# Reordering the gated feed-forward stage of a fused two-layer block: the second half's normalisation and weights pass ahead of the first half's epilogue

## What is computed

```
x = x + attn_like(layernorm(x))          # state-space mixer, then GELU MLP
x = x + ffn(layernorm(x))                # gated feed-forward

attn_like(x):
    xn = layernorm(x)*w + b
    gate, gate_gate = silu(xn @ gate_w + gate_b) split in two
    u = (xn*gate) @ state_w + state_b ;  Bm = gate_gate @ state_w + state_b
    delta = softplus(mean(xn @ state_w + state_b))
    y[t] = exp(-delta)*y[t-1] + delta*Bm*u
    x = x + y @ out_w + out_b
    return x + gelu(layernorm(x) @ mlp_w1 + b1) @ mlp_w2 + b2

ffn(x):                                   # weights are int, times 1/127
    h = silu(x @ w_gate.T) * (x @ w_up.T)           # hidden width 3072
    return h @ w_down.T
```

## Time and profile before

| what | value |
|---|---|
| runs shown | 7316.8 us and 8023.67 us, median 7670.24 us |
| profiled execution, its own time | 7320.83 us |
| span of its slowest core (core 6) | 7319.0 us |
| spans of the eight cores | 7274.2 to 7319.0 us |
| PE busy | 5569.8 us, 76% of the span |
| DVE busy | 2215.0 us, 30% |
| ACT busy | 1357.7 us, 19% |
| mean granted TensorE clock | 0.911 to 0.916 of full |

### The profile page before, as it was taken

The page is one execution under the profiler, slowest core; times in us unless marked ns, Lnnn a source line. Parts: engine busy times, 40 slices in busy tenths (PEclk is TensorE's granted clock), DMA queues, the critical chain, the costliest instruction groups (busy, mean ns, idle before and its releaser), DMA issues.

```text
span 7319.0 us, 70654 instructions; the slowest of 8 cores (7274.2 to 7319.0 us)
## 1 busy us (share of the span) xinstructions
PE 5569.8 (76%) x25312; PEld 2644.4 (36%) x25792; DVE 2215.0 (30%) x3924; ACT 1357.7 (19%) x1880; POOL 13.1 (0%) x28
## 2 busy tenths in 40 slices
PE   0027788769887688877888698877888778886988
PEld 0013344324433344433443344333444334433443
DVE  0024123340344213441233403442134502334033
ACT  0012111222112211121112221122112221122211
POOL 0000000000000000000000000000000000000000
PEclk9998899889998899988999799988999889987999
DMA  9940324211341124402242114411244022421143
GB/s 108 109 93 24 104 82 134 106 69 53 123 151 54 64 80 124 147 23 104 82 133 108 69 58 122 157 44 74 70 131 140 24 104 90 140 93 69 64 125 123
DMA packets 161078, 690.51 MB, mean 94 GB/s; under 512 B 18978, under 2 KB 19107, under 8 KB 134820
## 3 DMA queue, kind: packets, MB, share of 16 engines
q1 hardware_dynamic: 156964, 608.37, 25.3%
q0 software_dynamic: 3776, 77.60, 6.5%
HBM read 696.38 MB, written 77.59 MB: 106 GB/s over the span
## 4 chain that ended last, share of the span: by engine, by line
PE 69%; DVE 11%; DMA 6%; another core or an unknown queue 6%; issue 5%; ACT 3%; DVEq 0%; SPq 0%; ACTq 0%; POOL 0%; POOLq 0%
PE pb L334 27%; PE pb L916 12%; PE pb L1100 9%; PE pb L1088 9%; PE pb L1179 7%; DMA REG<-s_mlp 3%; PE pb L386 2%; DMA REG<-s_fd 2%; PE pb L413 2%; DVE REG L731 1%; ACT TTR L1019 1%; PE pb L668 1%; DVE X L777 1%; DVE TTR L779 1%
## 5 line engine op out<-in xcount | busy, mean ns | idle before, releaser
L334 PE MATMUL pb<-FMB,REG 128*128 128x512 bf16 x4000 | 895.0, 384 | 321.6 <-DMA REG<-s_mlp 314.5
L386 PE MATMUL pb<-IDF,TTR 128*128 128x128 f32 x1536 | 293.9, 342 | 861.8 <-DVE TTR L510 501.0
L916 PE MATMUL pb<-M1R,TTR 128*128 128x512 bf16 x4016 | 884.2, 379 | 14.1 <-ACT M1R L350 8.8
L334 PE MATMUL pb<-REG,M1R 128*128 128x512 bf16 x3008 | 701.5, 394 | 144.7 <-DVE REG L737 140.0
L1179 PE MATMUL pb<-M1R,REG 128*128 128x512 bf16 x3008 | 688.3, 387 | 71.8 <-DMA REG<-s_fd 46.8
L1088 PE MATMUL pb<-FMB,REG 128*128 128x512 bf16 x3008 | 719.7, 379 | 21.1 <-DVE FMB L1034 18.5
L1100 PE MATMUL pb<-FMB,REG 128*128 128x512 bf16 x3008 | 719.7, 379 | 3.5
L334 PEld LDWEIGHTS pb<-FMB,REG 128*128 128x128 bf16 x4096 | 403.7, 99 | 809.1 <-issue 339.5
L932 DVE TENSOR_SCALAR TTR<-pb,CB_M 128x512 f32<-128x512 f32 x128 | 96.1, 751 | 1977.5 <-PE pb L916 1977.5
L916 PEld LDWEIGHTS pb<-M1R,TTR 128*128 128x128 bf16 x4096 | 400.6, 98 | 495.0 <-issue 16.8
L386 PEld LDWEIGHTS pb<-IDF,TTR 128*128 128x128 f32 x1536 | 217.6, 175 | 938.7 <-issue 928.5
(11 more groups left out here) (97 smaller groups left out, 2938.6 us busy)
## 6 DMA issues: line engine op xcount, KB each, us to landing
TTR<-s_mlp SPq DMA_DIRECT2D x128, 1024.0 KB, 4.9
REG<-s_fg SPq DMA_DIRECT2D x384, 256.0 KB, 2.7
REG<-s_fu SPq DMA_DIRECT2D x384, 256.0 KB, 2.7
REG<-s_fd SPq DMA_DIRECT2D x128, 768.0 KB, 4.5
TTR<-x_in SPq DMA_DIRECT2D x16, 2048.0 KB, 8.9
M1R<-s_gate SPq DMA_DIRECT2D x8, 4096.0 KB, 12.8
y_out<-X POOLq DMA_DIRECT2D x16, 2048.0 KB, 6.6
s_mlp<-w_mlp POOLq DMA_DIRECT2D x2, 8192.0 KB, 175.6
```

The lines of the kernel that those rows point to most:

```text
L334: ins = t.matmul(psum[bank][:, 0:512], wsb[:, w_tile(m, k) * P:(w_tile(m, k) + 1) * P], rhs_fn(s, k), start=(k == 0), stop=(k == n_k - 1))
L386: ins = t.transpose(psum[bank][:, tau * P:(tau + 1) * P], src[:, tau * 1024 + c * P: tau * 1024 + (c + 1) * P], IDF[:])
L916: ins = t.matmul(psum[bank][:, 0:512], A_RING[:, slot + k * P:slot + (k + 1) * P], M1[:, k * 512:(k + 1) * 512], start=(k == 0), stop=(k = ...
```

## The change

```diff
-            for s in range(NSUB):
+            def emit_ln3(s, t2_free):
...
-                    for mk in reg_free["T2"]:
+                    for mk in t2_free:
...
+            def emit_gu(s, zn_marks, m1_free):
...
-                    if s == 0:
-                        pr.waits(t, "pe", reg_free["M1"])
+                    pr.waits(t, "pe", m1_free)
...
                         if m > 0:
                             pr.wait(ac, "act", ("dve", dve_base3 + (m - 1) * 2 + 2))
+                        elif CM.get(f"hlast{b}_{1 - s}") is not None and s == 1:
+                            pr.wait(ac, "act", CM[f"hlast{b}_0"])
...
                         pr.wait(dv, "dve", CM[f"fuf{b}_{s}_{m}"])
+                        if s == 1 and m == 0:
+                            pr.wait(dv, "dve", CM[f"fdf{b}_0_{ND - 1}"])
...
-                if s == 1 and b + 1 < n_blocks:
-                    emit_A_chain(b + 1, 0, defer_x1gen=False)
...
-                if s == 1 and b + 1 < n_blocks:
-                    wmix_free_next = pr.mark("pe")
-                    reg_free["FMB"] = [ffn_gu_done]
-                    emit_A_tail_sub(b + 1, 0, pending_xn[0])
-                    emit_A_chain(b + 1, 1, defer_x1gen=True)
...
+            emit_ln3(0, reg_free["T2"])
+            zn0, _ = emit_zn(0)
+            h0 = emit_gu(0, zn0, reg_free["M1"])
+            emit_ln3(1, [pr.mark("pe")])
+            zn1, _ = emit_zn(1)
+            d0base = emit_down(0, h0)
+            ffno0 = emit_fev4(0, d0base)
+            h1 = emit_gu(1, zn1, [])
+            ffn_gu_done = pr.mark("pe")
+            if b + 1 < n_blocks:
+                emit_A_chain(b + 1, 0, defer_x1gen=True)
+            emit_ffn_tail(0, ffno0)
+            if b + 1 < n_blocks:
+                emit_X1gen(b + 1, 0)
+            d1base = emit_down(1, h1)
+            ffno1 = emit_fev4(1, d1base)
+            if b + 1 < n_blocks:
+                wmix_free_next = pr.mark("pe")
+                reg_free["FMB"] = [ffn_gu_done]
+                emit_A_tail_sub(b + 1, 0, pending_xn[0])
+                emit_A_chain(b + 1, 1, defer_x1gen=True)
+            emit_ffn_tail(1, ffno1)
+            reg_free["M1"] = [pr.mark("pe")]
+            if b + 1 < n_blocks:
+                emit_X1gen(b + 1, 1)
+                emit_A_tail_sub(b + 1, 1, pending_xn[1])
```

More of the change, by code:

```diff
@@ L982, in build_program @@
             rds = [12288, 15360]
-            for s in range(NSUB):
+            ringslots_d = rds
+            def emit_ln3(s, t2_free):
                 def fv7(dv, s=s):
@@ L1010, in build_program, with fa8 @@
                 dve_sec(fv7)
-                def fa8(ac, s=s):
+                def fa8(ac, s=s, t2_free=t2_free):
                     pr.wait(ac, "act", CM[f"ln3c{b}_{s}"])
-                    for mk in reg_free["T2"]:
+                    for mk in t2_free:
                         pr.wait(ac, "act", mk)
@@ L1025, in build_program, with emit_zn @@
                 act_sec(fa8)
+            def emit_zn(s):
                 fills4 = tm_to_fm_pe(T2, [CM[f"t3{b}_{s}"]], "dve")
@@ L1040, in build_program @@
                 dve_sec(fev_zn)
-                reg_free["T2"] = [pr.mark("pe")]
+                return zn_marks, pr.mark("pe")
+            def emit_gu(s, zn_marks, m1_free):
                 pe_base3 = pr.c["pe"]
@@ L1106, in build_program @@
                 pe_sec(fpe3)
-                if s == 1:
-                    ffn_gu_done = pr.mark("pe")
                 def fact3(ac, s=s, dve_base3=dve_base3):
@@ L1140, in build_program @@
                 assert pr.c["dve"] == dve_base3 + 2 * NM_FFN
+                CM[f"hlast{b}_{s}"] = h_marks[-1]
                 prev_g[0] = CM[f"fgf{b}_{s}_{NM_FFN - 2}"]
@@ L1144, in build_program, with emit_down @@
                 prev_u[1] = CM[f"fuf{b}_{s}_{NM_FFN - 1}"]
-                if s == 1 and b + 1 < n_blocks:
-                    emit_A_chain(b + 1, 0, defer_x1gen=False)
+                return h_marks
+            def emit_down(s, h_marks, extra_pe=()):
                 pe_base4 = pr.c["pe"]
-                dve_base4 = pr.c["dve"]
                 def frd(sy, s=s):
@@ L1165, in build_program @@
                 sync_sec(frd)
+                dve_base4 = pr.c["dve"]
                 def fpe4(t, s=s, dve_base4=dve_base4):
                     pr.waits(t, "pe", h_marks)
+                    for mk in extra_pe:
+                        pr.wait(t, "pe", mk)
                     for m in range(ND):
@@ L1186, in build_program, with emit_fev4 @@
                 prev_d[1] = CM[f"fdf{b}_{s}_{ND - 1}"]
+                return dve_base4
+            def emit_fev4(s, dve_base4):
                 ffno_marks = []
@@ L1201, in build_program, with emit_ffn_tail @@
                 assert pr.c["dve"] == dve_base4 + ND
-                if s == 1 and b + 1 < n_blocks:
-                    wmix_free_next = pr.mark("pe")
-                    reg_free["FMB"] = [ffn_gu_done]
-                    emit_A_tail_sub(b + 1, 0, pending_xn[0])
-                    emit_A_chain(b + 1, 1, defer_x1gen=True)
+                return ffno_marks
+            def emit_ffn_tail(s, ffno_marks):
                 fills5 = fm_to_tm_pe(A_FFNO, ffno_marks, "dve", 1)
```

## The result

The changed kernel takes 1.0133 times as long as the kernel before, with a 95% interval of 1.0112 to 1.0153: slower by 1.3%, and within the 2% band. Of its 11 runs the five lowest took 7407 to 7431 us, beside 7315 to 7324 us for the kernel before. The profiled execution of the changed kernel has a span of 7414.4 us on its slowest core against 7319.0, 95 us more.

What follows compares the result with a forecast made beforehand. PE's work plus its stalls for other engines bound the kernel. Per block 91.4 us added minus 76.4 removed gave +15.0, times seven, minus 5 in the last: +100 on 7320.83, so 7420 us; range 7382 to 7468.

Steps and rivals of the forecast that it cites:

- GU(0) to zn(1), 17.6 us: Between GU(0) and zn(1): PE stands 17.6 us for LN3(1), because its consumer zn(1) is queued ahead of D(0).
- D(0) to GU(1), nothing: Between D(0) and GU(1): 23.5 us before becomes nothing if weights are there; bound 3 us.
- D(0) itself stays as it is: First half's down projection: no change in its own time, so no term for it.
- GU(1) to D(1), 29.3 us: Between GU(1) and D(1): PE waits for A(0) ahead of tail(0), 28.6 us, plus 0.7 for late x_in.
- D(1), 44.5 us: Second half's down projection: 44.5 us, including 0.7 for x_in and the clock; bounds 41.5 and 47.
- the slower rival: Store and x_in bite: over 2% slower, taking a store over 18 us or x_in 7 us late per block; 9%.
- X1gen(0), hidden: After tail(0): DVE needs about 10.5 us, including 7.5 for the store, hidden behind D(1)'s first four groups, 21 us.
- The clock: Start of D(1): may begin at the lower clock after the stall, at worst 1.5 us; 0.4 included in 44.5.
- bound of 73 us: Whole span: estimated most that clock ramps could add, from the skill page's under 1%; the rows allowed about 10.
- No wait of D(1) for line 1194: Expected sign in a middle block: D(1) never waits for line 1194; such a wait would make that step wrong.
- The last block, 5 us less: Last block, which has no A(0): loses 28.6 us and gains 23.5, so -5.
- The faster one: Rival at GU(1) to D(1): PE need not stand for A(0), 20.5 us less per block, about 7277 us; 3%.

Runs made afterwards that it cites:

- the woven run: Changed kernel with tail(0) emitted ahead of A(0) and LN3(1) cut into 14 DVE portions inside GU(0), DVE doing ACT's scaling: 7126.8 us, ratio 0.9776.
- tail(0) first: Changed kernel with one pair of calls swapped, tail(0) emitted ahead of A(0), X1gen(0) still behind A(0): 7271.1 us, ratio 0.9938.
- the last three kernels: Tail(0) ahead of A(0) with LN3(1) woven into GU(0), 0.9776; plus LN3(0) early, 7038.5 us; plus A(0), A(1) beside D(0), D(1), 0.9564.

## Why the prediction was right or wrong, point by point

*The time and its range: wrong.* The median over all 11 runs of the changed kernel is 7523 us, outside 7382 to 7468. The step that failed is the last one of the sum, where the text sets the median of 7670 aside, because it is the mean of 7317 and 8024, and lets the sum stand against the lower of the two. The runs showed that the higher kind is the commoner: six of the 11 took 7523 to 8185 us, so the median is one of these, and of the kernel before seven of ten took 7499 to 8223. A range for the median had to allow for that. Against the lower times alone the sum was sound: the five lowest are 7407 to 7431 us beside the forecast of 7420, and the ratio, 1.0133, is next to the 1.4% of the sum. The upper bound is a slip besides: its own terms add to 7420 + 46 = 7466, not 7468; nothing hangs on it.

*GU(0) to zn(1), 17.6 us: right.* 17.74 in block 1, 17.5 to 17.9 in all. The normalisation that was moved ahead of D(0) is exposed behind GU(0) instead, as the run with it moved back and the woven run show from both sides.

*D(0) to GU(1), nothing: right.* GU(1)'s first matmul starts at 2066.49, as the last one of D(0) ends; the weights were there.

*"D(0) itself stays as it is": not so.* From its first matmul to the end of its last it took 43.9 us in the mean of seven blocks before and takes 42.2 us now. Two rows, of block 5 before and block 3 after, show the greater part:

```profile
5391.22 12.21 PE L1179 MATMUL pb<-M1R,REG 128*128 128x512 bf16 x47 [1.99 <-DVE M1R L1135]
...
3761.05 41.75 PE L1187 MATMUL pb<-M1R,REG 128*128 128x512 bf16 x192
```

Before, D(0) stood behind a wait of 1.98 us for the last `h`, and in five of the seven blocks its first matmuls ran slower for it, 12.21 us for 47 instead of 10.52; in block 2 the granted clock was 0.80 and then 0.58 over the first 5.2 us. Now D(0) follows the transposes of zn(1) at once and starts at full speed in every block, and its weights are on time more often. The sum had no term for this; it is 1.6 us per block in favour of the change.

*GU(1) to D(1), 29.3 us: right.* GU(1) ends at 2149.53 and D(1) starts at 2179.33: 29.8 us, with 1.17 us of it a late `x_in`. Over the seven blocks it is 27.9 to 30.4 us, 28.8 in the mean.

*D(1), 44.5 us: 1 us short.* From its start to At(0) it took 43.4 us in block 0 (1309.88 to 1353.30), 47.6 in block 1 and 47.4 in block 6 (6508.19 to 6555.63), 45.5 in the mean of seven. The prediction put the store beside the third group's weights only in the slower rival, where it was to bite from 18 us on. It does bite, but in another way: by making that load late, 1.85 us in the mean, as the run without the store shows.

*X1gen(0), hidden: right.* DVE waits 8.27 us for the store, where 7.5 were expected, and is done with `X1` as `fev4(1)` begins at 2191.50, well before the fifth group of D(1) needs it.

*The clock: it falls in the stall, but the cost lies elsewhere.* D(1) was expected perhaps to begin at the lower level. Windows of the changed kernel, block 1 (busy us by engine, then granted clock, DMA share, GB/s):

```profile
2149.50:2173.80 24.30, 0.91 (x10) 0.70 (x8) 18.64 (x58) 0.00 (x0) 0.00 (x0) 0.62 0.17 72
2173.80:2179.30 5.50, 5.33 (x24) 4.30 (x25) 3.45 (x6) 0.00 (x0) 0.00 (x0) 0.52 0.00 0
2179.30:2184.00 4.70, 4.70 (x24) 2.17 (x23) 1.03 (x2) 0.00 (x0) 0.53 (x1) 1.00 0.50 209
```

The clock falls during the stall (0.62 in the mean of it), is near 1.2 GHz through the rest of the transposes and at 2.4 GHz when D(1) begins, so the loss there is 0, in all seven blocks. It is lost later: behind the 2.04 us wait the next 48 matmuls take 12.21 us in place of 10.52. This happens in three blocks, 4.8 us in all. The Trainium skill's advice against idle gaps ("TensorE: Matmul & The Clock Gate", Why this matters for your kernels) agrees with the trace in that the granted clock falls in the gap; but the long new gap cost nothing in clock and a short one did. The 4.8 us lie far below the bound of 73 us drawn from that page.

*"No wait of D(1) for line 1194": the row says otherwise, the code does not.* The changed kernel shows waits of D(1) put down to line 1204, 0.93 and 1.05 us in block 1. By `fpe4`, group 4, the fifth, waits for two things: the evacuation of group 0, which ended at 2192.2 at the latest, 12.8 us before group 4 starts at 2205.03, and its weights. So by elimination it was the weights. The traffic fits: from 2200.0 to 2204.1 the DMA moved 189 GB/s, about 775 KB and so one group's 768 KB, and from 2204.3 on nothing. The profile puts the wait down to the event that came last, and line 1204 had just ended an instruction, at 2204.90, that group 4 does not need. In the run with tail(0) first the same row, 2.30 us, is a real one: there line 1204's first evacuations run from 2158.60 and the group starts at 2159.42.

*The last block, 5 us less: right.* From zn(0) to the end of the span it is 7414.4 - 7107.17 = 307.2 us, against 7319.0 - 7006.05 = 313.0. The seven others, from zn(0) to zn(0), take (7107.17 - 1037.99) / 7 = 867.0 us against (7006.05 - 1037.00) / 7 = 852.7: 14.3 more, for 15.0. That this is so near is in part luck: D(1) was 1.0 us longer than its term, and D(0) 1.6 and the edge ahead of D(1) 0.5 shorter.

*The rivals.* The faster one named the point from which it would hold, A(0) exposed by under 5.5 us. With tail(0) first that exposure is 2.3 us in block 1, and the kernel is indeed faster, by 0.6%. The Trainium skill's remark on interleaving ("Perfetto Trace Analysis", Optimization Strategy) agrees with the last three kernels and not with the changed one: interleaving paid where the serial chain was laid beside independent matmuls.

## What to carry to other kernels

When engines work their queues in order, putting a piece earlier hides it only if PE finds, behind the point where the piece runs on the other engine, work that doesn't need it. So for each moved piece write down who stands behind it in every queue. LN3(1) was moved together with the transposes that need it, and its stall only changed place. A(0) kept its place, but tail(0), which doesn't need it, was put behind it on DVE, and the matmuls of D(1), which need neither, stood behind tail(0) on PE: so a chain of 20.5 us that had been hidden stopped PE in full. A long chain of small instructions is best cut into portions that fit the slack of a steady loop: cut so, the 16 us chain left the loop beside it at its 83.04 us.

## What the runs showed of the hardware that was not expected

A pause of PE of 22 to 24 us with 5.5 us of transposes behind it left the following matmuls at the full clock, in all seven blocks. Short waits inside or ahead of dense matmuls did cost, but not always. In D(1) of the changed kernel the waits ahead of the third group were followed by matmuls at full speed in four blocks (0.58, 1.03, 1.28 and 1.35 us) and by 48 matmuls in 11.89 to 12.21 us in place of 10.52 in three (2.04, 2.69 and 4.00 us). But the length of the wait doesn't settle it: with tail(0) first a wait of 2.30 us was followed by 48 matmuls in 10.52 us, and in the woven kernel one of 2.22 us by 72 in 17.39 us in place of 15.70. What decides was not tested.
